# A decoder layer on one core: the cross-attention queries are split once and laid out by DMA instead of by eight products, and VectorE takes a score tile in the first unit

## The reference

```python
x = x + self_attention(layernorm(x))             # 16 heads of 8, causal
x = x + cross_attention(layernorm(x), ctx_768)   # 16 heads of 8, 6404 keys
x = x + experts(layernorm(x))                    # 8 experts of 512, the best 2 per row

q = query @ Wq + bq                              # cross attention
attn = softmax(clip(einsum(q, k) * 8 ** -0.5))
x = einsum(attn, v) @ Wo + bo
```

## Time and profile before

| | |
|---|---|
| median of 3 runs | 931.27 us (927.54 to 932.93) |
| the profiled execution | 927.39 us |
| its span in the profile | 925.7 us |
| TensorE (PE) busy | 853.8 us, 92% |
| ScalarE (ACT) busy | 828.1 us, 89% |
| VectorE (DVE) busy | 494.5 us, 53% |
| mean granted clock of TensorE | 0.991 |

### The profile page before, as it was taken

One profiled execution on the slowest core, in us unless ns is written; L12 is line 12 of the kernel. 1 busy time (PEld: TensorE's weight loads), 2 busy tenths in 40 slices (PEclk: granted clock), 3 DMA queues, 4 the chain that ended last, 5 costly groups with the idle time before them and its releaser, 6 DMA issues.

```text
span 925.7 us, 15997 instructions
## 1 busy us (share of the span) xinstructions
PE 853.8 (92%) x6253; PEld 267.9 (29%) x6253; DVE 494.5 (53%) x975; ACT 828.1 (89%) x688; POOL 47.5 (5%) x104
## 2 busy tenths in 40 slices
PE   6987879999899989999989999999999999999997
PEld 4652222222222222222222232232222222223543
DVE  5665543421587678777875127355535554644432
ACT  5677978999999999999999999999999999998442
POOL 4000000000000000000000013000000000001300
PEclk9989999999999999999999999999999999999999
DMA  4661017411211212121111124122223210102120
GB/s 153 213 229 57 2 22 222 125 35 35 38 38 35 51 34 46 43 45 38 35 35 39 38 41 133 45 60 58 58 61 60 57 59 23 47 23 78 36 103 13
DMA packets 26670, 59.30 MB, mean 64 GB/s; under 512 B 7306, under 2 KB 12404, under 8 KB 26332
## 3 DMA queue, kind: packets, MB, share of 16 engines
q1 hardware_dynamic: 23132, 47.33, 19.7%
q0 software_dynamic: 3456, 10.88, 3.7%
HBM read 39.69 MB, written 10.64 MB: 54 GB/s over the span
## 4 chain that ended last, share of the span: by engine, by line
PE 53%; ACT 28%; issue 13%; DVE 4%; DMA 0%; SPq 0%; ACTq 0%; DVEq 0%
ACT probs L941 28%; PE psum L1798 22%; PE psum L1762 11%; PE psum L2097 3%; PE psum L2105 3%; PE psum L1741 2%; PE psum L1653 1%; PE psum L2042 1%; PE psum L1734 1%; PE psum L1657 1%; PE psum L1919 1%; DVE turned L1189 1%; PE psum L2035 1%; PE psum L1794 1%; PE psum L1613 1%
## 5 line engine op out<-in xcount | busy, mean ns | idle before, releaser
L941 ACT ACTIVATE probs<-psum 128x1536 f32<-128x1536 f32 x562 | 765.0, 1530 | 27.4 <-PE psum L1762 16.0
L1798 PE MATMUL psum<-probs,v_ctx 128*9 128x512 f32 x3080 | 403.0, 595 | 2.9 <-DVE turned L1189 2.9
L1762 PE MATMUL psum<-q_all,k_ring 32*128 32x512 f32 (+1 forms) x1732 | 282.7, 487 | 48.6 <-ACT probs L941 43.9
L1762 PEld LDWEIGHTS psum<-q_all,k_ring 32*128 32x128 f32 x1732 | 108.5, 182 | 399.4 <-ACT probs L941 355.1
L1232 DVE TENSOR_SCALAR attnT<-psum 128x512 f32<-128x512 f32 x60 | 41.5, 692 | 127.4 <-PE psum L1734 126.9
L1798 PEld LDWEIGHTS psum<-probs,v_ctx 128*9 128x9 f32 x3080 | 45.9, 88 | 99.1 <-issue 93.5
L1013 ACT ACTIVATE probs<-psum,b_sb 128x512 f32<-128x512 f32 x32 | 22.0, 687 | 34.0 <-PE psum L2097 34.0
L1189 DVE STREAM_TRANSPOSE turned<-psum 128x512 f32<-128x512 f32 x16 | 11.5, 717 | 72.3 <-PE psum L1794 57.2
L1243 DVE SCALAR_TENSOR_TENSOR kparts_bc<-kparts_bc,attnT 128x512 f32<-128x512 f32 x60 | 41.5, 692 | 2.0
L1233 DVE SCALAR_TENSOR_TENSOR attnT<-attnT,psum 128x512 f32<-128x512 f32 x60 | 41.2, 687 | 2.0
L1798 PE MATMUL psum<-probs,v_self 128*9 128x512 f32 (+3 forms) x384 | 40.3, 519 | 1.8 <-DVE probs L1210 1.2
(11 more groups left out here) (251 smaller groups left out, 611.2 us busy)
## 6 DMA issues: line engine op xcount, KB each, us to landing
k_ring<-kc_parts SPq DMA_DIRECT2D x256, 52.0 KB
k_ring<-kc_parts SPq DMA_DIRECT2D x256, 48.0 KB
kc_parts<-kparts_bc SPq DMA_DIRECT2D x8, 512.0 KB, 3.9
q_all<-w_region POOLq DMA_DIRECT2D x13, 256.0 KB, 2.7
q_all<-ctx_region POOLq DMA_DIRECT2D x13, 256.0 KB, 2.8
kc_parts<-probs SPq DMA_DIRECT2D x4, 512.0 KB, 3.9
w_region<-in_L_ffn_W SPq DMA_DIRECT2D x1, 2048.0 KB, 8.9
probs<-gate_rows SPq DMA_DIRECT2D x2, 1024.0 KB, 5.7
```

Of the source, the lines that this page charges most:

```text
L941: act.activation(probs[:, slot:slot + w, :], psum[:, at:at + w, :], ACT.Exp, scale=SC[ph]).then_inc(L[ph]["exp_done"], 1)
L1762: mm = pe.matmul(into[:, col:col + n_q], keys, q_all[rows, g, hf * HALF + q0:hf * HALF + q0 + n_q], start=True, stop=True)
L1798: mm = pe.matmul(into[:, q0:q0 + w], v_all[:, h, t, :], probs[:, place(ph, at)[1], col:col + w], start=first, stop=last)
```

## The change

- The eight `quad_queries` products are gone, and with them the wide weights, the biases on quad rows (16 small loads at the start) and VectorE's three operations on each.
- In their place VectorE splits the plain queries of a half once (`queries`), and SyncE stores the two parts to a buffer in DRAM and loads them back on the rows of all four quads, with 16 transfers (`load_queries`), once per half. For the first half this happens in self-attention, for the second in the first unit.
- TensorE waits for the first reload before cross group 0 and for the second before `tail_scores(1)`.
- On SyncE the second reload stands ahead of the experts' weights; piece load 5 is put ahead of both.
- The norms move from group 42 to 26, the columns from 45 to 29, the second tail from 37 to 35, and the end of the fixed part from 52 to 40.
- Tile 45 of the first unit goes to VectorE (lanes at groups 42, 47, 52 and 57, sums at 64). The cross-attention has 1536 banks in 512 groups, where it had 1540 in 514 (the last of one bank).

```diff
-VECTOR_OF = {1: (15, 30, 45), 2: (15, 30, 45), 3: (15, 30, 45), 5: (30, 45), 6: (30, 45), 7: (30, 45)}
+VECTOR_OF = {0: (45,), 1: (15, 30, 45), 2: (15, 30, 45), 3: (15, 30, 45), 5: (30, 45), 6: (30, 45), 7: (30, 45)}
...
-QUADS_AT = (None, 1, 4, 7, 25, 28, 31, 34)
-PROJ_AT, ROWS_AT, PLAIN_AT = 13, 19, 22
-TAIL_AT = (10, 37)
-NORMS_AT, COLUMNS_AT = 42, 45
-CLEAR_AT = 52
+PROJ_AT, ROWS_AT, PLAIN_AT, NORMS_AT, COLUMNS_AT = 13, 19, 22, 26, 29
+TAIL_AT = (10, 35)
+CLEAR_AT = 40
...
+            def load_queries(hf):
+
+                here = slice(hf * HALF, (hf + 1) * HALF)
+                sp.wait_ge(s["qquad_split"], hf + 1)
+                for part, src in enumerate((x_high, x_low)):
+                    sp.dma_start(qx_dram[part, :, here], src).then_inc(s["q_stored"], 16)
+                sp.wait_ge(s["q_stored"], 16 * PARTS * (hf + 1))
+                for r in range(LANES):
+                    for j in range(COPIES):
+                        row = ROWS * r + HD * j
+                        sp.dma_start(q_all[row:row + HD, :, here].bitcast(F32),
+                                     qx_dram[j % 2, :, here].rearrange("(g r d) c -> r d g c", g=QUADS, r=LANES)[r])\
+                            .then_inc(s["q_loaded"], 16)
...
+            early = [load for load in range(PIECE_RING, LOADS) if piece_scored(load - PIECE_RING) <= PART_AT]
+            before_queries = [load for load in early if piece_scored(load - PIECE_RING) <= PLAIN_AT]
+            load_pieces(before_queries)
+            load_queries(1)
...
-                if c == 8:
-                    act.wait_ge(s["wlate_loaded"], 16 * LATE)
-                    quad_weights(2, wq_sb[:, :], [sign * QUERY_SCALE for sign in Q_SIGNS], s["wcross_quads"])
...
                 dve.wait_ge(s["qcross_ps"], hf + 1)
-                step(dve.tensor_scalar(x_plain, bank(SIDE_BANK), bq_sb[:, 0:1], None, ALU.add), "qquad_step")
-                step(dve.tensor_tensor(sq_x[:, hf * HALF:(hf + 1) * HALF], x_plain, x_plain, ALU.mult), "sq_cross")
+                step(dve.tensor_scalar(x_plain, bank(SIDE_BANK), bq_sb[:, 0:1], QUERY_SCALE, ALU.add, ALU.mult), "qquad_step")
+                if hf == 1:
+                    step(dve.tensor_tensor(sq_x[:, hf * HALF:(hf + 1) * HALF], x_plain, x_plain, ALU.mult), "sq_cross")
+                step(dve.tensor_copy(x_high.bitcast(F32R), x_plain), "qquad_step")
+                step(dve.tensor_tensor(x_low.bitcast(F32R), x_plain, x_high, ALU.subtract), "qquad_split")
+                if hf == 0:
+                    step(dve.tensor_tensor(sq_x[:, hf * HALF:(hf + 1) * HALF], x_plain, x_plain, ALU.mult), "sq_cross")
...
+                if ph == 1 and group == 0:
+                    pe.wait_ge(s["q_loaded"], 16 * LANES * COPIES)
...
             def tail_scores(hf):
                 pe.wait_ge(s["ktail_made"], 1)
-                pe.wait_ge(s["qquad_split"], QUADS * (hf + 1))
+                pe.wait_ge(s["q_loaded"], 16 * LANES * COPIES * (hf + 1))
```

More of the change, by code:

```diff
@@ L275, in vector_plan @@
     for unit, tiles in VECTOR_OF.items():
-        at = ends[unit - 1] + 1 if unit < QUADS else max(lanes) + 1
+        at = (ends[unit - 1] if unit else PART_AT) + 1 if unit < QUADS else max(lanes) + 1
         for t in tiles:
@@ L590, in _ @@
                     sp.dma_start(dst[rows, :], src.rearrange("(g r d) n -> r g d n", g=QUADS, r=LANES)[r])\
[L591 to L594, removed]
                         .then_inc(s["wlate_loaded"], 16)
@@ L691, in _, with load_pieces @@
                 load_piece(load)
+            def load_pieces(loads):
+                for load in loads:
+                    sp.wait_ge(L[1]["qk_done"], piece_scored(load - PIECE_RING))
+                    load_piece(load)
+            early = [load for load in range(PIECE_RING, LOADS) if piece_scored(load - PIECE_RING) <= PART_AT]
+            before_queries = [load for load in early if piece_scored(load - PIECE_RING) <= PLAIN_AT]
+            load_pieces(before_queries)
+            load_queries(1)
             sp.wait_ge(s["tail_done"], 1)
@@ L700, in _ @@
                 .then_inc(s["xs_cleared"], 16)
[L702 to L708, removed]
+            load_pieces(early[len(before_queries):])
             def load_general_cross():
@@ L1062, in _ @@
             step(dve.tensor_copy(low[:, :], row_bit[:, :]))
-            step(dve.tensor_scalar(q_sign[:, :], low[:, 0:1], 2.0, -1.0, ALU.mult, ALU.add))
             for hf in range(NHALF):
@@ L1256, in normalise @@
                         for group in sorted(VECTOR_LANES):
-                            if n and ends[n - 1][3] <= group < ends[n][3]:
+                            if (ends[n - 1][3] if n else 0) <= group < ends[n][3]:
                                 vector_lane(group)
@@ L1367, in general_rows @@
                     alone(ins)
-            def first_half_mean():
-                signed_biases()
-                residual(0, 0, SIDE_BANK)
-            first_half = {FIRST_HALF + 1: first_half_mean, FIRST_HALF + 8: lambda: normalise_rows(0),
-                          FIRST_HALF + 12: lambda: rows_turned(0), FIRST_HALF + 16: lambda: query_squares(0),
-                          FIRST_HALF + 19: lambda: query_parts(0)}
+            first_half = {FIRST_HALF + 1: lambda: residual(0, 0, SIDE_BANK), FIRST_HALF + 8: lambda: normalise_rows(0),
+                          FIRST_HALF + 12: lambda: rows_turned(0), FIRST_HALF + 16: lambda: queries(0)}
             before = dict(made)
@@ L1395, in _ @@
                               ALU.mult).then_inc(s["ktail_made"], 1)
-            for m in range(1, QUADS):
-                query_parts(m)
             residual(0, 1, SIDE_BANK)
@@ L1400, in _ @@
             rows_turned(1)
-            query_squares(1)
-            for m in range(QUADS, 2 * QUADS):
-                query_parts(m)
+            queries(1)
             dve.wait_ge(s["norms_done"], 3)
@@ L1974, in _ @@
                            PLAIN_AT: lambda: plain_queries(1), NORMS_AT: norms_of_queries, COLUMNS_AT: columns_of_queries,
-                           CLEAR_AT: lambda: pe.wait_ge(s["bounded_made"], 2)}
-            for m in range(1, 2 * QUADS):
-                second_half[QUADS_AT[m]] = lambda m=m: quad_queries(m)
+                           CLEAR_AT: lambda: pe.wait_ge(s["tail_exp"], 2)}
             for hf in range(NHALF):
```

44 lines of the change are left out of this document (15 added, 29 removed).

## The result

The changed kernel is slower on this chip: 935.11 us median of 20 runs, against 931.04 of 20 runs of the kernel before on the same chip. The ratio is 1.0058, with a 95% interval of 1.0039 to 1.0077. The forecast was 924.7 us. On another chip the same pair gave 935.27 against 931.73 us; there three executions at 939 to 941 us were left out of the ratio as disturbed, which makes it 0.9995 (0.9964 to 1.0025) and the median of the other nine 932.6, while five at 941 to 944 us stayed in the first ratio. So the change costs between nothing and 0.8%, and doesn't bring the 6.6 us.

A forecast was written before the change was run, and what follows sets the result against it. The first unit was taken as bound by TensorE's side work, the rest by ScalarE's banks. Gains of 1.2 + 3.6 + 1.8 = 6.6 us off the 931.3 us median gave 924.7 us, range 919.5 to 930.5.

The forecast's parts named there:

- With 3.1 us for the last one to land this is 8.9 us: Either reload's duration: 5.75 us to issue 16 transfers, plus 3.1 us for the last to land.
- It fits with 0.8 us to spare.: Second reload, first unit: ready after 17.1 us, wanted by TensorE at group 35 after 17.9; cost 0.
- So it is hidden, with 4.1 us to spare.: First reload, in self-attention: landed at 128.4, before TensorE scores cross group 0 at 132.5; cost 0.
- Rival D: Both reloads long, 0.95 us per transfer: 5.4 and 8.7 us late, 938.8 us in all; chance 0.05.
- The rule on transfers: For a 1 MB reload: about 2 us fixed plus bytes at 436 GB/s, 4.4 us instead of 8.9.
- SyncE's other work. Cost 0.: Experts' weights going out some 35 us later on SyncE, and the next piece load, would cost nothing.
- The sum of 6.6 us: Whole gain forecast: 1.2 in self-attention, 3.6 from the first unit's products, 1.8 from VectorE's tile.
- The 1.2 us in self-attention: Removing the product there ends ScalarE's idle 0.44 and 0.76 us; 1.2 us won, bounds 0 and 1.8.
- The 3.6 us in the first unit: Removing seven products there wins 3.6 of 4.63 us of ScalarE gaps; bounds 1.0 and 4.6.
- The tile: First unit's tile moved to VectorE: four banks fewer for ScalarE, 1.8 us won, bounds 1.3 and 1.8.
- B: Second reload a little late at group 35, 3 us beyond ScalarE's reserve: 927.7 us; chance 0.12.
- C: First unit's gaps stay because TensorE's clock falls or stays low without the products: 928.3 or 929.5 us; chance 0.23.

The follow-up runs named there:

- e1: The changed kernel, with SyncE waiting for the second reload to land before it issues the experts' weights: 929.9 us, ratio 1.0018.
- e4: The kernel before with the first half's part alone, products 0 to 3 giving way to one reload: 926.4 us, ratio 0.9975.
- e9: The changed kernel with each reload as 8 transfers onto 16 partitions instead of 16 onto 8, weights still behind: 928.0 us, ratio 0.9947.
- e5: e2 with each reload as 8 transfers onto 16 partitions instead of 16 onto 8: 924.9 us, ratio 0.9938.
- e7: e5 plus three TensorE products without a use at the change of stages: 924.7 us, ratio 0.9927.
- e13: e5 plus 11 waits on a load at TensorE's start: 920.4 us, ratio 0.9930.
- e14: The changed kernel plus 11 waits on a load at TensorE's start: 931.7 us, ratio 1.0037.
- e8: e2 without VectorE's tile, second tail at group 45, fixed part's end at 50, and the 16 small bias loads back: 928.1 us, ratio 0.9973.
- e2: The changed kernel with the experts' weights and the clearing sent ahead of piece load 5 and the second reload: 929.2 us, ratio 1.0008.
- e11: The changed kernel unaltered, run again beside others on one chip: 935.3 us, ratio 0.9995 to the kernel before.
- e12: e5 plus 10 waits on a load at the end of TensorE's program: 925.1 us, ratio 0.9975.

## Why the prediction was wrong

**The step that failed: the second reload.** "With 3.1 us for the last one to land this is 8.9 us" and hence "It fits with 0.8 us to spare." The counting around it was right. The plain queries' product starts at 176.80, VectorE 1.2 us later, the passes end 2.7 us after that (3.0 forecast), the stores take 2.7 (4 forecast), and TensorE wants the queries 18.25 us after the product (17.9 forecast). The reload took 17.5 us, 15.7 of them by its own rate (e1) and some 2 by the transfers behind it. I took the time to issue 16 transfers, 5.75 us, for the time to move them. It only bounds it from below: the same 16 issues took 6.02 us here.

The transfers that I had read it from did land in the time that I allowed. They are the `k_ring<-self_parts` of the earlier trace rows, issued from 58.13 us, also 16 of 64 KB onto 8 partitions in pieces of 2 KB; by the DMA records their last piece ends at 66.1 us, 8.0 us after the first issue. Two windows of them, in the kernel before:

```profile
62.00:64.00 2.00, 1.99 (x14) 0.18 (x11) 2.00 (x7) 1.81 (x2) 0.00 (x0) 0.50 0.56 148
64.00:66.00 2.00, 2.00 (x20) 0.81 (x21) 0.47 (x2) 1.19 (x1) 0.00 (x0) 0.51 0.53 153
```

That is twice the reload's rate at the same share, so neither the pieces nor the number of partitions alone makes the reload slow. What differs is that the rows of `query_parts` stand 4 KB apart in DRAM and those of `self_parts` 2 KB, the order in which the copies read the two parts, and the destination. None of these was tested.

**"So it is hidden, with 4.1 us to spare."** The first reload failed by the same step: 14.3 to 14.9 us in five profiles (e4's text), where 8.9 were counted. After, it took 11.4 us and was in time.

**Rival D** had the right outcome by a wrong reading. Its 0.95 us is the longest time that SyncE took to issue one transfer, not the time of a transfer: the issues of the slow reloads took 0.30 us each in the middle and 0.88 at most. That 16 times 0.95, 15.2 us, comes near the 15.7 measured is luck. What it said holds at the second reload, 8.6 us longer than forecast where D had 9.5. At the first TensorE was 0.9 to 1.6 us late in five profiles of nine, against its 5.4. So D's price of 14.1 us was too high.

**The rule on transfers.** The Trainium skill's page "DMA: Bandwidth & Descriptors", section "Anatomy of one DMA", gave 4.4 us for a reload as an estimate. Its figures are for transfers that GpSimd issues, and SyncE issues these. Measured were 15.7 us on 8 partitions and under 10.5 on 16 (from 179.16 to 189.67, where TensorE doesn't wait). The row that spoke against the page was right to do so, and not strong enough.

**"SyncE's other work. Cost 0."** Wrong while the reload is slow (7.56 against 5.84 and 5.40 us), right once it is fast (e9).

**The sum of 6.6 us** stands up where the reload is out of the way. The median spans of e5, e7, e9 and e13 lie 7.9, 6.0, 5.9 and 7.7 us under before's. The 1.2 us in self-attention: from the exponential behind the gap of 0.44 us to the first of cross-attention it is 22.98 us before (114.17 to 137.15) and 21.62 in e9 (115.95 to 137.57), 1.4 us less. The 0.44 itself stays (0.43 in e9), so that the sum comes out near 1.2 is partly luck. The 3.6 us in the first unit: in e9 only 0.51, 0.38 and 0.52 us are left there, so all 4.6 can go. The tile: 1.8 or more by the medians, not resolved.

**What the sum left out.** It took "what lies around" the span as fixed. It grew by 2.2 us in the changed kernel, which is a third of the forecast gain, and the padding of e13 and e14 takes it away.

**Rivals B and C.** B's mechanism is D's, with too small a size. C's low clock appears in some profiles (gaps of 0.82 and 1.10 us near 150 us after, none in e9). In e4 and e8 it falls after TensorE stood for the first reload, and after the change at the second: the clock is 0.50 when the tail products come (2.04 us against 1.19 in e5). In e2 and e5 it falls at 138 us although the reload was in time. So part of it follows from the reload, and part is scatter.

**The account of the medians** (e11's series): span 931.1 against 929.8, +1.3; outside +2.2. With the forecast's -6.6 the reload's gap, 7.1 to 7.6 us beyond the usual 0.5, gives +0.5 to +1.0 in the span; the rest is within the scatter. With the nine executions of the result the span is 928.9, 0.9 us under before's; what the first reload and the start cost in the median isn't known. So the account fits, and isn't proven.

**Open.** Why a reload moves 73 to 93 GB/s in most profiles and 98 to 102 at the first reload after, why the transfers of the same shape in the kernel before moved about 150, and by what mechanism TensorE's instruction count sets the program's end. The runs show that they do, not why.

## What to carry to other kernels

The time to issue DMAs is a lower bound of the time until they have landed, and the durations of the issuing instructions say nothing of the transfers. A rate read from transfers with the same pieces and the same number of partitions can still be off by two (150 and 78 GB/s here), so a load that something waits for wants more room than 0.8 us, or a small run of its own. A transfer laid on twice the partitions finished in under 70% of the time here, for a change of one loop. Where a wait is put down to an engine, ask whether that engine was done before: at cross group 0 the row names ScalarE, and it was the reload. Compare each run's time less its span too: two microseconds appeared there, and a few instructions at the start of one engine's program took them away.

## What was not expected of the hardware

**Half the DMA engines.** Transfers onto 8 partitions kept the share at about 0.5 of 16 engines (0.49 to 0.58), and those onto 16 partitions at 1.05 to 1.08. But the piece loads of before, 8 partitions too with pieces of 6 KB, moved twice as much at the same share:

```profile
146.00:148.00 2.00, 2.00 (x13) 0.48 (x5) 0.00 (x0) 2.00 (x2) 0.00 (x0) 1.00 0.51 163
```

163 GB/s against 78, and the pieces of 2 KB from `self_parts` 148 and 153: the share doesn't say how much is moved. The reload of e5 moved only 127 GB/s at a share of 1.07.

**A program's end that depends on an engine's instruction count.** 1.7 us outside the span with 4845 TensorE instructions or more, 3.0 with 4836 and 3.9 to 4.1 with 4840, over the runs of the table on four chips. It isn't a matter of more or less alone: 4836 has less outside than 4840.

**One more place of gaps.** After and e5 to e11 show gaps somewhere from 552 to 568 us, 1.4 to 4 us in sum, which before, e1 to e4 and e12 to e14 don't. So it goes by the series of runs, each on its chip, more than by the kernel. In e9 TensorE first waits 2.25 us there, and then the clock is at the lower level:

```profile
555.49 0.51 PE L1760 MATMUL psum<-q_all,k_ring 32*128 32x512 f32 x3 [2.25 <-ACT probs L951]
```

```profile
558.00:560.00 2.00, 2.00 (x11) 0.13 (x8) 0.00 (x0) 2.00 (x2) 0.00 (x0) 0.50 0.58 134
```
